# A two-layer graph network on one core: the last 32 chunks of layer 0 as two groups of 16, and a finished block's work inside its own group

## The chip, the cores and the metric

The kernel runs on 1 core of one Trainium2 chip. The metric is the device time of one execution in microseconds (us); the median of the runs is given. The core's engines are TensorE (PE; PEld is its weight load), VectorE (DVE), ScalarE (ACT), GpSimd (POOL) and SyncE (SP, here only DMA issues). Each runs its own instructions in order and waits on semaphores for the others.

## What is computed

There are 3750 nodes with 256 features and 120,000 edges in order of their target `dst`, which is uneven (3750 u^2). Two layers follow each other; in between only the residual `x` is kept.

```python
def _L0_gnn_ref(inputs, conv_weights, attn_l, attn_r, h_bias, edge_src, edge_dst, edge_type):
    feat_all = jnp.einsum('ni,rhid->rnhd', inputs, conv_weights)      # 8 relations, 4 heads of 64
    feat_src_e = feat_all[edge_type, edge_src]
    feat_dst_e = feat_all[edge_type, edge_dst]
    el = jnp.sum(feat_src_e * attn_l[edge_type], axis=-1)
    er = jnp.sum(feat_dst_e * attn_r[edge_type], axis=-1)
    e = jax.nn.leaky_relu(el + er, negative_slope=LEAKY_SLOPE)
    m = jax.ops.segment_max(e, edge_dst, num_segments=N_NODES)
    ex = jnp.exp(e - m[edge_dst])
    denom = jax.ops.segment_sum(ex, edge_dst, num_segments=N_NODES)
    alpha = ex / denom[edge_dst]
    h = jax.ops.segment_sum(alpha[..., None] * feat_src_e, edge_dst, num_segments=N_NODES)
    return h.reshape(N_NODES, OUT_FEAT) + h_bias
...
h = jnp.maximum(_layernorm(x, axis=-1), 0.0)
x = x + _L0_gnn_ref(h, L0_gnn_conv_weights, ..., src, dst, edge_type_8)
h = jnp.maximum(_layernorm(x, axis=-1), 0.0)
x = x + _L1_gnn_ref(h, src, dst, edge_type_8, ...)   # messages h @ W[type] summed by target, h @ loop_w, gelu, layernorm
```

## The kernel before

**Stages.** (1) The first norm, the features of every node for the 8 relations, stored as rows of `tab0`, and the tables of edges, sorted into chunks. (2) Layer 0 over the edges. (3) Layer 1 over the edges, from `tab1`. POOL's indirect DMAs (L843) fetch the rows of one chunk of 128 edges each.

**Layer 0.** The 30 blocks of 128 target nodes (`NB`) are in order of their number of edges, smallest first, and lie side by side in `ACC`. Their 996 chunks are taken in 32 groups (`GROUPS`): one of 4 chunks, 31 of `G` = 32. Two groups' rows fit into `Z` (`FE`), so POOL fetches one group while the engines work on the one before. `fetch` waits at chunks 0, 8, 16 and 24 of a group for semaphores of PE: select done (`s_es`), pairs done (`s_pair`), scores done (`s_sc`).

In one turn of the group loop, for group g:
- DVE, `attend(g)`: adds the two halves of the scores (`EV`, L1397), which needs the group's rows and select(g); PE transposes them (L2037); DVE scans for the maxima along the edges (L1410, L1412), PE transposes the two results (L2040), DVE scans over the chunks (RV, L1419, to L1448), PE spreads the result (L2044), DVE scans again, ACT takes Exp (EX, L1792), PE transposes it (L2048). With these weights `scale_rows` (L1383, 8 chunks at a time) multiplies the fetched rows.
- PE, `late`/`weigh` (L1889): one product with a one-hot matrix for each pair of chunks, into a ring of four PSUM banks (0, 1, 6, 7); a pair waits until DVE has added (`add`, L1355) the pair four before it into `ACC`. Pairs 0 to 3 of a group run in its own turn, 4 to 15 in the next turn, in the gaps of `attend`; `cuts(g)` says how DVE's adds are spread over them. `rescale` corrects the running sums of the block.
- For group g + 1: ACT turns the loaded targets into a one-hot (`turned`, two long activations) and copies the `er` rows (`stage`), PE makes `scores`, DVE picks the types (`types`, ERM, L1364), PE sums them (`select`, L1970), DVE makes one-hots (`onehot0`, L1373).
- Block r = g - 4 is finished (`finished_in`): DVE divides by the sums, adds bias and `x`, and norms it (`finish`, L1488 to L897, with the square root of ACT in between, L1631), ACT takes the Relu (`normed`, L1754). In the same turn PE flips it (`flip_block`, L1991, bank 3) and ACT moves it to `HT` (L1759). Its products with layer 1's weights (`block_products`: four quarters of 512 columns, L2006, in banks 2 and 3, then the own product L2009 to L2013) run a turn later, behind select; ACT moves each quarter to `ST1` (L1741) and the own product to `ACC` (L1746), SP stores the quarters into `tab1` (`store_table`).

PE's order at the end of a turn is: scores, pairs 0 to 3, select(g + 1), products of block r - 1, flip of block r. Behind the last group come block 26's leftovers, the turning back of layer 1's places (`TD`, `ERM`, fetched by 16 gathers of POOL, L858 and L859, once the last select is over), and blocks 27, 28 and 29, one behind the other. Layer 1's first gather waits for all stores into `tab1` and for `KI`.

## Time and profile before

| | us |
|---|---|
| runs (3): lowest, median, highest | 2775.06, 2777.38, 2780.21 |
| profiled execution, its own time | 2783.18 |
| its span, first to last instruction | 2781.4 |
| busy in the span: PE, DVE, ACT, POOL | 1935.2, 1523.3, 675.1, 2025.8 |
| mean granted TensorE clock | 0.809 of 2.4 GHz |

Shares and groups are of that one execution. In the rows below the first number is the start in us from the span's start, the second the time of the row in us; "xN" is the number of instructions merged in the row; the bracket at the end is the engine's idle time before it and what ended it. `Z` holds the gathered rows, `PB` is PSUM.

### The profile page before, as it was taken

Reading aid. Unit: us, or ns where it says so; the run is one execution under the profiler, and the core shown is the slowest. Engines: PE = TensorE matmul, PEld = TensorE weight load, DVE = VectorE, ACT = ScalarE, POOL = GpSimd, SP = SyncE. Lnnn points to the kernel's source line nnn. Section 1 sums busy time; section 2 is a strip of 40 time slices with the busy share of each in tenths; the row PEclk is TensorE's granted clock in tenths of the full one; section 3 lists DMA queues with packets and bytes.
Section 4 is the critical chain, followed back from the end, with each engine's and each line's share of the span. In section 5 each row is a group of like instructions: output and inputs, shape, how many; then the busy total and the mean of one; then the engine's idle time right before and its main releaser. Section 6 shows DMA issues by size and latency. Waiting matters only on the chain.

```text
span 2781.4 us, 26396 instructions
## 1 busy us (share of the span) xinstructions
PE 1935.2 (70%) x8092; PEld 1435.2 (52%) x8092; DVE 1523.3 (55%) x3170; ACT 675.1 (24%) x1248; POOL 2025.8 (73%) x2138
## 2 busy tenths in 40 slices
PE   7993567887878888798878556565555656556564
PEld 6982355555655555565555344444444444444443
DVE  7754677777778777777776333323332332333233
ACT  4653333444344434434432100000000000000001
POOL 5956777777777777777774577777777777777775
PEclk9995678889888988888899877768677676777767
DMA  8557455566665656565652533333333333333333
GB/s 244 206 192 223 145 146 166 168 171 178 179 169 166 185 166 176 170 181 168 170 162 86 163 105 105 105 110 106 110 105 110 111 105 110 106 110 109 107 112 93
DMA packets 168504, 403.11 MB, mean 145 GB/s; under 512 B 49741, under 2 KB 75820, under 8 KB 160682
## 3 DMA queue, kind: packets, MB, share of 16 engines
q0 software_dynamic: 95312, 261.58, 35.0%
q1 hardware_dynamic: 73050, 139.85, 14.5%
q8 instruction: 64, 1.05, 0.2%
q14 instruction: 78, 0.64, 0.1%
HBM read 325.41 MB, written 75.86 MB: 144 GB/s over the span
## 4 chain that ended last, share of the span: by engine, by line
POOL 58%; issue 19%; PE 11%; DVE 7%; DMA 2%; ACT 1%; DVEq 0%; POOLq 0%; SPq 0%; ACTq 0%
POOL Z L843 54%; PE PB L1889 4%; PE PB L2006 3%; DVE Z L1383 2%; DVE ACC L1355 2%; POOL ACC L804 2%; DMA Z<-tab,KI 1%; PE PB L1841 1%; POOL Z L807 1%; PE PB L1970 1%; POOL Z L801 0%; PE PB L2011 0%; DVE ERM L1364 0%; ACT L1631 0%; DMA Z<-in_L_gnn_basis 0%
## 5 line engine op out<-in xcount | busy, mean ns | idle before, releaser
L843 POOL DMA_INDIRECT Z<-tab,KI x1963 | 1866.6, 951 | 654.0 <-issue 591.6
L1889 PE MATMUL PB<-Z,OHZ 128*128 128x260 f32 (+1 forms) x3926 | 1199.2, 469 | 521.5 <-DMA Z<-tab,KI 392.2
L1889 PEld LDWEIGHTS PB<-Z,OHZ 128*128 128x128 f32 x3926 | 910.2, 239 | 756.4 <-DMA Z<-tab,KI 413.8
L1355 DVE TENSOR_TENSOR ACC<-ACC,PB 128x260 f32 (+1 forms) x997 | 421.7, 423 | 849.9 <-PE PB L1889 826.1
L1383 DVE TENSOR_TENSOR Z<-Z,PB 128x2048 f32<-128x2048 f32 (+1 forms) x125 | 284.1, 2273 | 0.0
L2006 PE MATMUL PB<-w,ht 128*128 128x512 f32 x480 | 267.6, 721 | 1.8 <-ACT ht L1759 1.8
L1970 PE MATMUL PB<-pick,ERM 128*128 128x16 f32 (+1 forms) x504 | 111.7, 371 | 171.0 <-DVE ERM L1364 171.0
L1970 PEld LDWEIGHTS PB<-pick,ERM 128*128 128x128 f32 (+1 forms) x504 | 108.3, 326 | 184.1 <-DVE ERM L1364 184.1
L1821 ACT ACTIVATE ACC<-ACC 128x256 f32<-128x256 f32 x30 | 10.4, 406 | 778.5 <-DVE ACC L1355 778.5
L2006 PEld LDWEIGHTS PB<-w,ht 128*128 128x128 f32 x480 | 111.1, 238 | 136.2 <-issue 133.6
L1719 ACT ACTIVATE OHZ<-OHZ,kid 128x4096 bf16<-128x4096 bf16 (+1 forms) x32 | 115.7, 3616 | 214.3 <-DMA OHZ<-dlt 214.3
L1841 PE MATMUL PB<-wh,hx 128*128 128x424 f32 (+1 forms) x500 | 146.4, 364 | 3.4 <-ACT hx L1645 3.4
L1373 DVE TENSOR_TENSOR OHZ<-DL,PB 128x1024 f32<-128x1024 bf16 (+1 forms) x122 | 140.1, 1210 | 0.1
L1565 DVE TENSOR_TENSOR OHZ<-DL,PB 128x4096 f32<-128x4096 bf16 (+1 forms) x31 | 133.6, 4311 | 0.0
L1741 ACT ACTIVATE st<-PB 128x512 f32<-128x512 f32 x120 | 68.3, 590 | 268.4 <-PE PB L2006 268.4
L1721 ACT ACTIVATE OHZ<-OHZ,ones 128x4096 bf16<-128x4096 bf16 (+1 forms) x32 | 115.7, 3615 | 1.0
L1631 ACT ACTIVATE sd<-ve 128x1 f32<-128x1 f32 (+2 forms) x52 | 10.6, 204 | 428.0 <-DVE ve L1588 403.1
L1841 PEld LDWEIGHTS PB<-wh,hx 128*128 128x128 f32 x500 | 95.8, 192 | 7.3 <-ACT hx L1645 4.9
L1841 PE MATMUL PB<-wx,hx 128*128 128x424 f32 (+1 forms) x250 | 90.2, 361 | 0.0
L1733 ACT ACTIVATE ERG<-ER 128x96 bf16 x498 | 88.8, 266 | 0.1
L1397 DVE TENSOR_TENSOR EV<-Z,PB 128x128 f32<-128x128 f32 (+1 forms) x32 | 11.8, 369 | 134.4 <-DMA Z<-tab,KI 133.1
L895 DVE RECIPROCAL rs<-sd 128x1 f32<-128x1 f32 (+2 forms) x41 | 6.8, 167 | 131.5 <-ACT sd L1631 131.5
(336 smaller groups left out, 1566.9 us busy)
## 6 DMA issues: line engine op xcount, KB each, us to landing
OHZ<-dlt SPq DMA_DIRECT2D x31, 1024.0 KB
Z<-tab,KI POOLq DMA_INDIRECT x1963, 2.8
tab<-st SPq DMA_DIRECT2D x120, 256.0 KB, 2.9
tab<-Z SPq DMA_DIRECT2D x24, 1040.0 KB, 4.0
TD<-typ SPq DMA_DIRECT2D x31, 256.0 KB
tab<-Z SPq DMA_DIRECT2D x5, 1024.0 KB, 7.4
xn<-xb SPq DMA_DIRECT2D x30, 128.0 KB, 2.3
X<-xn SPq DMA_DIRECT2D x6, 640.0 KB, 9.4
```

The source lines that it names most:

```text
L843: pool.indirect_dma_start(to, None, tab, at).then_inc(d_fe[g % 2][part(g, k) * layer], 16)
L1355: dv.tensor_tensor(a, a, bank(done + i)[:, 0:width], ALU.add).wait_op(*previous, "sem-ge").then_inc(*o.of(s_add))
L1373: dv.tensor_tensor(OH[:, 0, c:c + w, :], DL[:, k0 + c:k0 + c + w].unsqueeze(2).to_broadcast([128, w, 128]), (iob[:, :] if c and g == NG - ...
L1383: dv.tensor_tensor(f, f, weights.unsqueeze(3).to_broadcast([128, w, 4, HD]), ALU.mult).then_inc(*o.of(s_sr))
L1565: dv.tensor_tensor(OH[:, g % 2, 0:n, :], DL[:, k0:k0 + n].unsqueeze(2).to_broadcast([128, n, 128]), lanes.unsqueeze(1).to_broadcast([128, ...
L1719: ac.activation(d, d, ACT.Abs, bias=kid[:, 0:1], scale=-1.0).then_inc(*o.of())
L1721: ac.activation(d, d, ACT.Relu, bias=ones[:, 0:1], scale=-1.0).then_inc(*o.of())
L1733: ac.activation(ERG[:, q, :].rearrange("p (i r) -> p i r", i=3), ER3[:, :, bass.ds(at[q], 32)], ACT.Copy).then_inc(*o.of(s_eg if q == n // ...
L1841: last = pe.matmul(to, hx[:, 128 * c:128 * c + 128], parts[u](c), start=(i == 0 and c == 0 and u == 0), stop=(i == 1 and c == 1))
L1889: last = pe.matmul(p, OH[:, slot, k + i, :], rows_, start=(i == 0), stop=(i == n - 1))
L1970: last = pe.matmul(to, ERM[0:32 * parts, 128 * j:128 * j + 128], pick[0:32 * parts, 0:4 * parts].rearrange("p (a h) -> p a h", h=4), start ...
L2006: last = pe.matmul(quarter_bank(j)[:, :], HT[:, c, :], W1[:, c, 512 * j:512 * j + 512], start=(c == 0), stop=(c == 1))
```

## The change

1. The last 32 chunks of layer 0 are two groups of 16 (33 groups in all); block 27 is finished in the first of them. Groups of 16 load their masks in four pieces.
2. A block finished in group g has all its work in turn g: DVE's `finish` is cut in two, the first half behind `rescale`, the second behind the second scale_rows and its three adds; PE runs flip and four products ahead of select(g + 1) and the own product behind it, then waits for its move. The quarters use the pairs' banks 0, 6, 7 and 1.
3. Pairs 4 and 5 run at the end of their own turn (`early`); the other pairs are spread anew (6 and 7, 8, 9 to 12, 13 to 15). DVE's adds keep their cuts. POOL's waits come at chunks 0, 4, 8, 16 and 24.
4. Behind the last group: blocks 28 and 29 only, their products back to back (`LATE` = 28, with `HTL`, three buffers for the flipped block, two of them over `FW`/`BW` and `MX`/`ZR`), then the turning back; DVE copies `KI` from PSUM (before: ACT to `TDF`, then POOL), and the own products come last.
5. Masks: two more operations for each of the two new borders, in the first stage.

```diff
+CUT0 = KT * 128 - G // 2
+GROUPS = [(PAD, G - PAD)] + [(k, G) for k in range(G, KT * 128 - G, G)] + [(CUT0 - G // 2, G // 2), (CUT0, G // 2)]
...
-            return 0 if GROUPS[g][1] <= 8 else 9 if g == NG - 1 else 4
+            return 0 if GROUPS[g][1] <= 8 else 3 if g == NG - 1 else 4
 
         def cuts(g):
 
-            return (6, 10, 14) if g == NG - 1 else (5, 8, 11)
+            return 5, 8, 11
+
+        def early(g):
+
+            return 6 if 0 < g < NG - 2 else 4
...
-            return g - 4
+            return g - 4 if g < LATE + 4 else -1
 
         def product_of(r, j):
 
-            return 5 * NB + 5 * r + j + 1
+            return 5 * NB + (5 * r if r < LATE else 4 * r + LATE) + j + 1
+
+        def own_product(r):
...
+        def flip_bank(r):
+
+            return PB[4 if r >= LATE else 1]
+
+        def quarter_bank(r, j):
+
+            return PB[2 + j % 2 if r >= LATE else (0, 6, 7, 1)[j]]
+
+        def own_bank(r):
+
+            return PB[2 + r - LATE if r >= LATE else 0]
+
+        def flipped(r):
+
+            return HTL[max(r - LATE, 0)]
...
-                if 0 <= r and g < NG - 1:
+                if 0 <= r < LATE:
                     store_block(r)
-                    if r:
-                        store_table(r - 1)
                     load_block(r + 2)
+                    store_table(r)
...
+                            pool.wait_ge(s_pair, min(pair_no(g - 2, 4), pair_no(g - 1, 0)))
+                        elif k == 4:
                             pool.wait_ge(s_es, g)
                         elif k == 8:
                             pool.wait_ge(s_pair, min(pair_no(g - 2, 8), pair_no(g - 1, 0)))
                         elif k == 16:
+                            pool.wait_ge(s_pair, min(pair_no(g - 2, 12), pair_no(g - 1, 0)))
+                        elif k == 24:
                             pool.wait_ge(s_pair, pair_no(g - 1, 0))
-                        elif k == 24:
                             pool.wait_ge(s_sc, scored(g, 0))
...
-            pool.wait_ge(s_kt, VISITS + 4)
-            pool.tensor_copy(KI[:, :], TDF).then_inc(*o.of(s_loc))
 
             for j in range(4):
                 pool.wait_ge(d_st[j], 16 * NB)
-            pool.wait_ge(s_loc, 5)
+            pool.wait_ge(s_ki, 2)
...
-                norm_scale(r, r + 1, FIN + r)
+                dv.wait_ge(*o.last())
+                dv.tensor_scalar(ve[:, r:r + 1], mv[:, r:r + 1, 1], 1e-5, None, ALU.add).then_inc(*o.of(s_ve))
+                yield
+                dv.wait_ge(s_sd, no)
+                dv.reciprocal(rs[:, r:r + 1], sd[:, r:r + 1]).then_inc(*o.of())
+                dv.wait_ge(*o.last())
+                dv.scalar_tensor_tensor(nmr[:, r:r + 1], mv[:, r:r + 1, 0], -1.0, rs[:, r:r + 1], ALU.mult,
+                                        ALU.mult).then_inc(*o.of(s_nm))
...
+                norm = finish(finished_in(g)) if finished_in(g) >= 0 else iter(())
+                next(norm, None)
                 for c in range(8, n, 8):
+                    if g == NG - 1:
+                        onehot0(g, c)
                     scale_rows(g, c)
                     if c == 8 or g == NG - 1:
                         for q in range(3 * (c // 8 - 1), 3 * (c // 8)):
                             add(q0 + q, ROW0, 0)
                     elif c == 16:
                         add(q0 + 3, ROW0, 0)
+                    if c == 8:
+                        next(norm, None)
+                if n == G // 2 and g + 1 < NG:
+                    add(q0 + 3, ROW0, 0)
                 if g + 1 < NG:
                     types(g + 1)
-                for c in range(8 if g + 1 < NG else 24, n, 8):
-                    onehot0(g, c)
                 if g + 1 < NG:
+                    for c in range(8, n, 8):
+                        onehot0(g, c)
                     onehot0(g + 1, 0)
                     load_places(g + 1)
-                if finished_in(g) >= 0:
-                    finish(finished_in(g))
             for q in range(added_in_turn(NG - 1), GROUPS[NG - 1][1] // 2):
                 add(pair_no(NG - 1, q), ROW0, 0)
-            finish(NB - 2)
-            finish(NB - 1)
+            for r in range(LATE, NB):
+                for _ in finish(r):
+                    pass
+            for i in range(2):
+                dv.wait_ge(s_pt, VISITS + i + 1)
+                dv.tensor_copy(KI[:, 512 * i:512 * i + 512], PB[6 + i][:, :]).then_inc(*o.of(s_ki))
...
+                r = finished_in(g - 1)
+                if r >= 0:
+                    for j in range(4):
+                        move_quarter(r, j)
+                    move_own(r)
+                if g + 1 < NG:
                     stage(g + 1)
-                r = finished_in(g - 1)
-                if r > 0:
-                    move_quarter(r - 1, 0)
-                    move_quarter(r - 1, 1)
-                if r >= 0:
-                    normed(r)
-                if r > 0:
-                    move_quarter(r - 1, 2)
-                    move_quarter(r - 1, 3)
-                    move_own(r - 1)
-                if r >= 0:
-                    move_flipped(r)
                 ac.wait_ge(s_z, g + 1)
                 ac.activation(fe, fz, ACT.Exp).then_inc(*o.of(s_fx))
                 ac.wait_ge(s_zr, g + 1)
                 ac.activation(EX[0:R, :], ZR[0:R, :], ACT.Exp).then_inc(*o.of(s_xr))
-
-            last = finished_in(NG - 1)
-            for j in range(4):
-                move_quarter(last - 1, j)
-            move_own(last - 1)
-            normed(last)
-            ac.wait_ge(s_oh, batch_no(NG - 1, G))
-            for i in range(2):
-                ac.wait_ge(s_pt, VISITS + i + 1)
-                ac.activation(DL[:, 512 * i:512 * i + 512], PB[2 + i][:, :], ACT.Copy).then_inc(*o.of(s_kt))
+                r = finished_in(g)
+                if r >= 0:
+                    normed(r)
+                    move_flipped(r)
+
+            normed(LATE)
+            move_flipped(LATE)
+            for r in range(LATE, NB):
+                move_quarter(r, 0)
+                if r + 1 < NB:
+                    normed(r + 1)
+                move_quarter(r, 1)
+                move_quarter(r, 2)
+                if r + 1 < NB:
+                    move_flipped(r + 1)
+                move_quarter(r, 3)
...
-                if r == finished_in(NG - 1):
-                    pe.wait_ge(s_kt, VISITS + 2)
-                pe.transpose(PB[3][:, 0:128], H0[:, 1, 0:128], ident[:, :])
-                pe.transpose(PB[3][:, 128:256], H0[:, 1, 128:256], ident[:, :]).then_inc(s_tr, 1)
+                if r < LATE:
+                    pe.wait_ge(s_add, pair_no(r + 4, 1))
+                to = flip_bank(r)
...
+                    if r < LATE and j < 3:
+                        pe.wait_ge(s_add, pair_no(r + 4, j + 2))
+                    if r >= LATE and j > 1:
                         pe.wait_ge(s_ev, moved(r, j - 2))
+                    elif r > LATE:
+                        pe.wait_ge(s_ev, moved(r - 1, j + 2))
+                    if LATE <= r < NB - 1 and j == 3:
+                        flip_block(r + 1)
...
+            def own_product_of(r):
+
+                h, to = flipped(r), own_bank(r)
+                pe.wait_ge(s_ev, moved(r, 0) if r < LATE else moved(NB - 1, 3))
+                pe.matmul(to[:, 0:D], ones[0:1, :], HB1[:, :], start=True, stop=False)
                 for c in range(2):
-                    pe.matmul(PB[2][:, 0:D], HT[:, c, :], LWS[:, c, :], start=False, stop=False)
+                    pe.matmul(to[:, 0:D], h[:, c, :], LWS[:, c, :], start=False, stop=False)
                 for c in range(2):
-                    last = pe.matmul(PB[2][:, 128 * c:128 * c + 128], HT[:, c, :], ident[:, :], start=False, stop=(c == 1))
+                    last = pe.matmul(to[:, 128 * c:128 * c + 128], h[:, c, :], ident[:, :], start=False, stop=(c == 1))
                 last.then_inc(s_mm, 1)
+
+            def turn_back(tile, banks):
+
+                for i in range(2):
+                    for t in range(4):
+                        last = pe.transpose(banks[i][:, 128 * t:128 * t + 128], tile(4 * i + t), ident[:, :])
+                    last.then_inc(s_pt, 1)
...
+                late(g - 1, early(g - 1), 8)
                 pe.wait_ge(s_pk, g + 1)
                 pe.transpose(PB[5][0:1, 0:R], PK[0:R, 0:1], ident[0:R, 0:R])
                 pe.transpose(PB[5][0:1, 128:128 + R], PK[0:R, 1:2], ident[0:R, 0:R]).then_inc(s_row, 1)
-                late(g - 1, *cuts(g)[0:2])
+                late(g - 1, 8, 9)
                 pe.wait_ge(s_cf, g + 1)
                 pe.matmul(PB[4][0:R, 256:257], CF[:, 0, 0:R], ones[0:1, 0:1], start=True, stop=True)
                 pe.matmul(PB[4][0:R, 257:258], CF[:, 1, 0:R], ones[0:1, 0:1], start=True, stop=True).then_inc(s_cc, 1)
-                late(g - 1, *cuts(g)[1:3])
+                late(g - 1, 9, 13)
                 pe.wait_ge(s_xr, g + 1)
                 pe.transpose(PB[5][:, 256:256 + R], EX[0:R, :], ident[0:R, 0:R]).then_inc(s_wt, 1)
                 if g:
                     pe.wait_ge(s_fm1, g)
                     pe.matmul(PB[4][:, 400:404], OH[0:1, 0, 0, :], fm, start=True, stop=True).then_inc(s_ff, 1)
-                late(g - 1, cuts(g)[2], 16)
+                late(g - 1, 13, 16)
                 if g + 1 < NG:
                     scores(g + 1, 0)
                 late(g, 0, 3)
                 if g + 1 < NG and halves(g + 1) > 1:
                     scores(g + 1, 1)
                 late(g, 3, 4)
+                r = finished_in(g)
+                if 0 <= r < LATE:
+                    flip_block(r)
+                    block_products(r)
                 if g + 1 < NG:
                     select(g + 1)
-                r = finished_in(g)
-                if r > 0:
-                    block_products(r - 1)
-                if r >= 0 and g + 1 < NG:
-                    flip_block(r)
+                if 0 <= r < LATE:
+                    own_product_of(r)
+                    pe.wait_ge(s_own, r + 1)
+                if g + 1 < NG:
+                    late(g, 4, early(g))
             late(NG - 1, 4, 16)
-
-            last = finished_in(NG - 1)
+            flip_block(LATE)
+            block_products(LATE)
+            block_products(LATE + 1)
             pe.wait_ge(s_loc, 4)
-            pe.wait_ge(s_own, last)
-            pe.wait_ge(s_ev, moved(last - 1, 3))
-            for i in range(4):
-                for t in range(4):
-                    tile = TD[:, 4 * i + t, :] if i < 2 else ERM[:, 512 * (i - 2) + 128 * t:512 * (i - 2) + 128 * t + 128]
-                    last = pe.transpose(PB[2 + i][:, 128 * t:128 * t + 128], tile, ident[:, :])
-                last.then_inc(s_pt, 1)
-
-            for r in range(finished_in(NG - 1), NB):
-                flip_block(r)
-                block_products(r)
-
             pe.wait_ge(s_add, NPAIR)
+            turn_back(lambda t: ERM[:, 128 * t:128 * t + 128], (PB[6], PB[7]))
+            turn_back(lambda t: TD[:, t, :], (PB[0], PB[1]))
+            for r in range(LATE, NB):
+                own_product_of(r)
```

## Rows read from the trace of the kernel before

**Rows 1.** Head of the page, and engines' shares of the chain that ended last
```profile
span 2781.4 us, 26396 instructions
...
POOL 58%; issue 19%; PE 11%; DVE 7%; DMA 2%; ACT 1%; DVEq 0%; POOLq 0%; SPq 0%; ACTq 0%
```

**Rows 2.** Waits: who waited for whom, us in total, times, longest
```profile
POOL Z L843 <- issue: 591.6, 1940, 0.3
```

**Rows 3.** Timeline of POOL: layer 0's first gather, the index gathers, layer 1's first
```profile
219.44 1.03 POOL L843 DMA_INDIRECT Z<-tab,KI  x1 [25.19 <-DMA tab<-Z]
...
1473.08 0.95 POOL L858 DMA_INDIRECT TD<-sdst,offi  x1 [0.31 <-issue]
...
1553.51 0.98 POOL L843 DMA_INDIRECT Z<-tab,KI  x1 [29.95 <-DMA tab<-st]
```

**Rows 4.** Timeline of a group in the body, first part, DVE and PE
```profile
1195.31 0.38 DVE L1397 TENSOR_TENSOR EV<-Z,PB 128x128 f32<-128x128 f32 x1 [2.79 <-DMA Z<-tab,KI]
...
1196.07 0.33 PE L2037 MATMUL PB<-IDX,E 128*128 128x128 f32 x1
...
1204.48 4.65 PE L1889 MATMUL PB<-Z,OHZ 128*128 128x260 f32 x20
...
1205.17 2.28 DVE L1383 TENSOR_TENSOR Z<-Z,PB 128x2048 f32<-128x2048 f32 x1
...
1210.34 2.29 DVE L1383 TENSOR_TENSOR Z<-Z,PB 128x2048 f32<-128x2048 f32 x1
...
1212.66 1.34 DVE L1355 TENSOR_TENSOR ACC<-ACC,PB 128x260 f32 x3
...
1213.46 1.14 PE L1889 MATMUL PB<-Z,OHZ 128*128 128x260 f32 x4
```

**Rows 5.** Timeline of the same group, second part
```profile
1220.23 3.59 PE L1970 MATMUL PB<-pick,ERM 128*128 128x16 f32 x16 [5.62 <-DVE ERM L1364]
...
1223.66 9.77 PE L2006 MATMUL PB<-w,ht 128*128 128x512 f32 x16
...
1224.73 0.18 DVE L1488 TENSOR_SCALAR dn<-ACC 128x4 f32<-128x4 f32 x1
...
1227.29 0.15 DVE L893 TENSOR_SCALAR ve<-mv 128x1 f32<-128x1 f32 x1
...
1232.18 0.16 DVE L895 RECIPROCAL rs<-sd 128x1 f32<-128x1 f32 x1 [4.74 <-ACT sd L1631]
...
1232.57 0.60 ACT L1754 ACTIVATE H<-xb,nmr,rs 128x256 f32<-128x256 f32 x1 [0.42 <-DVE nmr L897]
...
1233.71 0.69 PE L2009 MATMUL PB<-hb1s,ones 1*128 1x256 f32 x2 [0.28 <-ACT st L1741]
...
1235.94 0.39 ACT L1746 ACTIVATE ACC<-PB 128x256 f32<-128x256 f32 x1 [1.80 <-PE PB L2013]
```

**Rows 6.** Windows: length, busy of PE, PEld, DVE, ACT, POOL, then PEclk, DMA, GB/s
```profile
1218.00:1220.00 2.00, 0.00 (x0) 0.00 (x0) 2.00 (x3) 2.00 (x13) 1.39 (x3) 0.70 0.30 92
1220.00:1222.00 2.00, 1.77 (x9) 1.77 (x9) 2.00 (x3) 0.62 (x4) 1.60 (x2) 0.50 0.51 133
...
1229.00:1230.00 1.00, 1.00 (x4) 0.52 (x3) 0.00 (x0) 0.00 (x0) 0.69 (x2) 0.99 0.73 172
```

**Rows 7.** Timeline from the last group to the last product, DVE, PE and ACT
```profile
1475.73 0.37 DVE L1397 TENSOR_TENSOR EV<-Z,PB 128x128 f32<-128x128 f32 x1 [3.27 <-DMA Z<-tab,KI]
...
1519.99 0.43 DVE L1355 TENSOR_TENSOR ACC<-ACC,PB 128x260 f32 x1 [0.45 <-PE PB L1889]
...
1532.80 7.13 PE L2006 MATMUL PB<-w,ht 128*128 128x512 f32 x16 [0.53 <-ACT ht L1759]
...
1541.79 0.14 PEld L1991 LDWEIGHTS PB<-IDX,H 128*128 128x128 f32 x1
...
1542.81 7.13 PE L2006 MATMUL PB<-w,ht 128*128 128x512 f32 x16 [0.53 <-ACT ht L1759]
...
1549.98 0.60 ACT L1741 ACTIVATE st<-PB 128x512 f32<-128x512 f32 x1 [1.12 <-PE PB L2006]
```

81 lines of the change are left out of this document (30 added, 51 removed).

## The prediction

> **What bounds the kernel now.** I read the page's head and chain first [rows 1]: GpSimd (POOL) alone is 58% of the chain that ended last, and "issue" 19%. The waits put a name to that 19%: before 1940 of the 1963 gathers POOL waited for nothing but its own issue, 591.6 us, 0.305 each [rows 2]. POOL's timeline then cuts the run into three parts behind the first stage [rows 3]: layer 0's 996 gathers from 219.44 to 1473.1 us, 1.26 us each; a hole to 1553.51 us, in which POOL does 16 short gathers of indices and at last waits 29.95 us for a store of `tab`; then layer 1, gathers again. A group of 32 chunks takes POOL about 40.1 us, and DVE still has to wait 2.79 us for its last gathered row when it begins one [rows 4]. So the body of layer 0 goes at POOL's pace. A changed kernel can gain only in the hole of 80.4 us. It can lose there, and in the body if another engine comes to need more than 40.1 us for a group.
>
> **The body: a block's work inside its own group.** I cost it along one path. Let PE's transposes of the scores (L2037, 1196.07) be 0.
> (a) To the first scale_rows: 1205.17 - 1196.07 = 9.1 us now [rows 4]. In the new order two pairs of 0.93 us stand ahead of the row transposes instead of one (20 matmuls are 5 pairs in 4.65 us), and pair 12, now ahead of the transposes of EX, has to wait until DVE has added pair 8. I take 1.2 us for both: 10.3.
> (b) scale_rows, five adds, rescale (1205.17 to 1210.34) [rows 4]: 15.5.
> (c) The first half of finish comes here: 1224.73 to 1227.44, 2.7 us [rows 5]: 18.2.
> (d) scale_rows 2.3, three adds 1.35 [rows 4]: 21.9. The square root falls under it.
> (e) Reciprocal to the end of the Relu, 1232.18 to 1233.17, 1.0 us [rows 5]: 22.9.
> (f) Turning the block and moving it out, 1541.79 to 1542.81, and a semaphore, 1.1 us [rows 7]: 24.0.
> (g) Four products: 7.0 us at 2.4 GHz (7.13 in the row) [rows 7]. At 1.2 GHz each matmul takes twice as long, so every us spent at that clock adds half a us.
> (h) select, now behind them: 3.4 us between its start and the products', at a granted clock of 0.50 [rows 5, 6]. No row has it at the full clock; it can't be under half, 1.7, nor over 3.4. I take 2.1, nearer to half, because the products' matmuls do halve.
> (i) Own product and its move: 1233.71 to 1236.33, 2.6, with a semaphore 2.7 [rows 5]. PE now waits for this move; queued behind the wait are pairs 4 and 5 and the next group's transposes.
> (j) Pairs 4 and 5: 1.9 us.
> Sum: 24.0 + 7.0 + 2.1 + 2.7 + 1.9 = 37.7 us, plus half of the time at the low clock. Now PE stands still from 1214.6 to 1220.23, 5.62 us; the clock falls within 1218 to 1220, and is back at 1229.0, 5.3 us into the products [rows 4 to 6]. In the new order PE stands still for about 3.4 us, so the clock may fall or not: 0 to 5.3 us cold give 37.7 to 40.4, the middle 39.3. POOL's 40.1 still ends last, by 0.8 us. The path of the present order, worked out the same way (select at 24.1, products, own product, flips), needs 40.0, so the new one is no longer.
> What hides the rest: the quarters' moves on ACT wait behind the two long activations of turned() and end under select, since each quarter has a bank of its own. SP issues the table's stores in the same turn, behind the loads of masks, steps and targets and not in front of them, and the next masks are asked for only after the next transposes. POOL's waits come at chunks 0, 4, 8, 16 and 24; the tightest is select's, some 5 us ahead of its gather. Should the cover of 0.8 us go, its price is the excess times 27 groups. Body: 0; ends -2 (POOL's few short waits gone) and, with select at 3.4 us and the clock always low, 27 x 1.6 = +43 us.
>
> The clock is the doubtful term: the 3.4 us of select left it at 0.50, and it rose under the products [rows 5, 6]. The Trainium skill, "TensorE: Matmul & The Clock Gate", section "HAM oscillation — how this bites in real kernels", says that a loop in which the array waits in each turn restarts throttled in each turn. By that rule the products start cold in every group, which is the 40.4 of the sum and 0.3 us over POOL's pace; by the bare sum it is 37.7. The rule speaks against this change, which puts a wait for DVE and ACT right ahead of the dearest matmuls.
>
> **The hole: two groups of 16.** The last group of before starts at 1475.73 [rows 7]; the first of the two gets PE at about 1475.9.
> First group of 16: block 27 is finished in it, so its path is (a) to (i) again, 37.7 - 1.9, less 0.6 for vectors of half the width in (a) (an estimate: five or six short operations, 0.1 each), plus 1.6 for the clock: **36.8 us**. Half the chunks save gathers, half of the scale_rows, and pairs 4 and 5. DVE could go on near 28 us, but the next group's select stands behind block 27's products.
> Second group of 16: transposes to scale_rows 9.1 + 2.4 (four pairs ahead of the row transposes) - 0.9 = 10.6; scale_rows 2.3, rescale 0.6, a one-hot 1.2, scale_rows 2.3, three adds 1.35; pairs 4 to 7 at 0.9 each end 3.5 later: 21.8. PE idles for most of the first 13 us, so 1.0 for a low clock: **22.8 us**.
> From the last add to block 28's products: 2.7 of (c), 0.3 for the square root (an estimate, as long as a semaphore and a small operation of the rows), (e) and (f): 5.1. Products of 28 and 29 to the start of the last move: 7.35 (with the flip of 29 inside) + 7.17 (1542.81 to 1549.98) [rows 7] = 14.5. PE has stood still for 5 us before them: 4.4 us cold, 2.2. The move 0.6; from its end, 1550.58, to POOL's gather at 1553.51, 2.9 [rows 3, 7].
> Sum: 1475.9 + 36.8 + 22.8 + 5.1 + 14.5 + 2.2 + 0.6 + 2.9 = 1560.8 against 1553.5: **+7.3 us**. In words: now the last add starts at 1519.99 and three blocks of 10.0 us follow (1532.80 to 1542.81) [rows 7]. One block of the three goes, and 3.0 us between the others, but the last add comes 15 us later.
> Other queues: POOL's 16 index gathers wait for the last select, so they start near 1510 instead of at 1473.08 and are issued by 1530, 20 us early. DVE's two copies of the indices stand behind block 29's products; at 0.6 us each (the nearest row, a move of 512 columns) they end 1.3 us before the last store lands, and would be the bound at 1.3 us each. The masks' four new operations lie in the first stage. Ends of the hole: no cold clock at all, 4.8 less, +2.5; select at 3.4 us and up to twice the cold time, +12.
>
> **The time.** The profiled run took 2783.18 us, its span 2781.4 [rows 1]; the median of the runs shown is 2777.38, 5.8 less. With body 0 and hole +7.3 the profiled execution would take 2790.5 and the median is **2784.7**.
>
> **Rivals.**
> A, the body is lost to PE: select at 3.4 us, or the low clock coming back over pairs 4 to 7 after select, lifts a group over 40.1. It decides from 2.4 us beyond 37.7. At 0.5 to 1.5 us in 27 groups it gives +14 to +40 and, with the hole, 2798 to 2825. For it: the small slack. Against it: the present order has none by the same sum and holds POOL's pace.
> B, **faster**: the first group of 16 is not serial. If it takes under 24 us instead of 36.8, the hole shrinks by over 5.5 us: 2767 to 2772; break-even is 29.5. For it: the rows have landed long before, DVE could go on at 28 us, and 10.0 us of block 27 are really gone. Against it: PE's order is fixed, products, select, own product, and block 27's Relu would have to come 9 us earlier than in (e).
> C, within 0.2%: the clock stays high over the short waits, and the hole grows by 2.5 to 5 us: 2780 to 2782.5.
>
> **How the numbers follow.** About 0.2% (5.5 us) is what a measurement of this kernel can tell from no change. Forecast, +5.5 to +12: 0.40. C, with the small sums around it: 0.26. A: 0.20. B: 0.14. Hence faster 0.14, same 0.26, slower 0.60. The likeliest case alone reaches from 2783 to 2790. The range takes in much of A and B: 2772 to 2806.
>
> **What would show it.** Right, if: the gathers of layer 0 still follow each other at 1.25 us and end near 1473; L1397 is still released by gathered rows and not by select (else A); the products start about 24 us after the transposes; the last two groups' transposes are 37 us apart (B: 24); the last add is near 1535; two blocks follow instead of three; layer 1's first gather is near 1561 and released by a table store. Wrong, if the 37 us are not there, or if layer 1 waits for the indices.

## The result, and the profile after

The kernel before takes 2778.80 us beside it (4 runs, 2775.06 to 2783.59), the changed one 2807.76 us (4 runs, 2804.65 to 2810.87): ratio 1.010, 95% interval 1.0086 to 1.0114. The change costs 29 us, four times the forecast of 7.3, and lies just outside the range (2806). A second measurement gave the same ratio (g1_change, below). Rival A has come about in its size and its mark, on top of the hole that was forecast.

The profiled execution took 2805.64 us, its span is 2803.9. First the shares of the chain that ended last, of after; they answer to [rows 1]:

```profile
span 2803.9 us, 26507 instructions
...
POOL 37%; PE 30%; DVE 16%; issue 14%; ACT 2%; DMA 1%; DVEq 0%; POOLq 0%; SPq 0%; ACTq 0%
POOL Z L864 37%; PE PB L2033 10%; PE PB L1918 10%; PE PB L1870 5%; DVE Z L1405 5%; DVE ACC L1377 4%; PE PB L1994 2%; PE PB L2043 1%; PE PB L2041 1%; ACT H L1789 1%; PE PB L2045 0%; PE PB L2014 0%; DVE xb L1523 0%; DVE st L1525 0%; DVE H L1515 0%
```

POOL fell from 58% to 37% of the chain, PE rose from 11% to 30%; the products (L2033) and the pairs (L1918) are 10% each. The waits of after (who waited for whom, us in total, times, longest) say at which place; they answer to [rows 2] and to the wait in the first of [rows 4]:

```profile
DVE EV L1419 <- DMA Z<-tab,KI: 66.5, 10, 12.3
DVE EV L1419 <- PE PB L1994: 62.7, 23, 9.4
POOL Z L864 <- PE PB L1918: 34.4, 40, 9.1
POOL Z L864 <- issue: 585.4, 1919, 0.6
```

EV is DVE's first operation of a group. Before, the group's last gathered row released it [rows 4]; now in 23 groups it is select (L1994), which stands behind the finished block's products. The prediction named this very line as the mark of rival A.

A turn of after, PE's timeline (start us, us, engine, line, operation, out<-in, count, and what ended the idle time before). It answers to [rows 4, 5]:

```profile
1162.54 0.27 PE L2076 MATMUL PB<-IDX,E 128*128 128x128 f32 x1
...
1166.77 0.38 PE L2083 MATMUL PB<-ones,CF 1*128 1x1 f32 x2 [1.02 <-DVE CF L1459]
...
1167.91 5.46 PE L1918 MATMUL PB<-Z,OHZ 128*128 128x260 f32 x16 [0.54 <-DVE ACC L1377]
1173.21 0.27 PE L2087 MATMUL PB<-IDX,EX 128*128 128x128 f32 x1
...
1186.70 0.47 PE L2014 MATMUL PB<-IDX,H 128*128 128x128 f32 x1 [3.18 <-ACT H L1789]
1186.97 0.42 PE L2015 MATMUL PB<-IDX,H 128*128 128x128 f32 x1
1187.86 9.49 PE L2033 MATMUL PB<-w,ht 128*128 128x512 f32 x16 [0.47 <-ACT ht L1794]
1197.19 1.85 PE L1994 MATMUL PB<-pick,ERM 128*128 128x16 f32 x16
1198.97 0.69 PE L2041 MATMUL PB<-hb1s,ones 1*128 1x256 f32 x2
...
1201.64 2.02 PE L1918 MATMUL PB<-Z,OHZ 128*128 128x260 f32 x8 [0.47 <-ACT ACC L1781]
1203.50 0.27 PE L2076 MATMUL PB<-IDX,E 128*128 128x128 f32 x1
```

From transposes to transposes 40.96 us: 25.3 to the products, 9.3 to select, 1.8, 2.7 to pairs 4 and 5, 1.9. From group 13 on, seventeen turns in a row have 41.0 us each, to 0.1; before, the turns of the 30 full groups have 40.3 us in the mean and vary from 39.4 to 41.8. The windows of this turn (columns as in [rows 6]) show the clock:

```profile
1162.54:1185.90 23.36, 18.26 (x115) 13.49 (x113) 19.30 (x52) 5.01 (x16) 17.29 (x19) 0.93 0.57 168
1185.90:1192.60 6.70, 5.43 (x8) 2.45 (x9) 6.67 (x7) 5.74 (x4) 4.99 (x6) 0.50 0.49 133
1192.60:1203.50 10.90, 10.43 (x45) 6.83 (x45) 4.97 (x9) 6.13 (x13) 8.35 (x9) 1.00 0.67 200
```

TensorE stood still for 3.18 us ahead of the flip; the granted clock is 0.50 (1.2 GHz) from 1185.9 to 1192.6 and 1.00 (2.4 GHz) from there on, so 4.7 of the products' 9.3 us are at the lower level. DVE's timeline in the next turn gives step (a):

```profile
1214.79 0.16 DVE L1488 TENSOR_SCALAR F<-PB 128x4 f32<-128x4 f32 x1 [2.00 <-PE PB L2090]
...
1215.07 2.28 DVE L1405 TENSOR_TENSOR Z<-Z,PB 128x2048 f32<-128x2048 f32 x1
```

1215.07 - 1203.50 = 11.6 us from the transposes to the first scale_rows; 9.1 before [rows 4].

The clock is low a second time in the turn, and that time lies inside (a). Here is the stretch that holds most of pairs 9 to 12, first in the turn shown and then in a turn that begins at 713.20, in which the clock stayed high (columns as in [rows 6]); below them PE's rows for the same four pairs in that second turn, and DVE's first scale_rows:

```profile
1168.74:1172.16 3.42, 3.42 (x10) 2.65 (x9) 2.88 (x10) 1.59 (x2) 2.79 (x3) 0.50 0.48 104
718.60:722.60 4.00, 3.76 (x16) 2.99 (x17) 3.65 (x11) 1.50 (x2) 3.09 (x4) 1.00 0.48 103
```

```profile
718.57 2.90 PE L1918 MATMUL PB<-Z,OHZ 128*128 128x260 f32 x12 [0.54 <-DVE ACC L1377]
721.71 1.12 PE L1918 MATMUL PB<-Z,OHZ 128*128 128x260 f32 x4 [0.24 <-DVE ACC L1377]
...
723.56 2.28 DVE L1405 TENSOR_TENSOR Z<-Z,PB 128x2048 f32<-128x2048 f32 x1
```

At 2.4 GHz the 16 matmuls take 4.3 us (718.57 to 722.83), with a wait of 0.24 inside; in the turn above, at 0.50 for 3.4 us, they take 5.46. And 723.56 - 713.20 = 10.4 us is (a) at the full clock. That turn has 39.7 us in all, though its products are as slow (9.51).

The hole of after, all engines; it answers to [rows 3, 7]:

```profile
1524.80 1.95 PE L1994 MATMUL PB<-pick,ERM 64*128 64x8 f32 x16
...
1527.02 0.95 POOL L879 DMA_INDIRECT TD<-sdst,offi  x1 [23.10 <-PE PB L1994]
...
1530.82 0.30 PE L2076 MATMUL PB<-IDX,E 128*64 128x128 f32 x1 [0.47 <-ACT ACC L1781]
...
1553.13 0.42 DVE L1377 TENSOR_TENSOR ACC<-ACC,PB 128x260 f32 x1 [0.45 <-PE PB L1918]
...
1558.57 6.75 PE L2033 MATMUL PB<-w,ht 128*128 128x512 f32 x12 [0.47 <-ACT ht L1794]
...
1574.15 0.60 ACT L1776 ACTIVATE st<-PB 128x512 f32<-128x512 f32 x1 [1.12 <-PE PB L2033]
...
1577.68 0.97 POOL L864 DMA_INDIRECT Z<-tab,KI  x1 [26.18 <-DMA tab<-st]
```

The transposes of the first group of 16 are at 1491.9. From there to layer 1's first gather it takes 85.8 us, where before takes 77.0 from the last group's transposes (1476.5): the hole lost 8.8 us. Between the two spans (2781.4 and 2803.9, 22.5 apart) the books are: body of layer 0 +21.0, hole +8.8, the stage ahead of layer 0 -5.6 (its first gather is at 213.85 instead of 219.44, which nothing in the change explains), layer 1 -1.7. The medians are 29 apart, since that first stage varies: in g1_change, the same kernel, layer 0's first gather is at 218.6.

### The profile page after: what moved, and what is told of

It is laid out like the page before. It is cut to its first block, busy times and chain, and to the rows that moved or that the text cites. A ratio compares the mean times of both kernels' runs of the same rounds, so it can differ in the third digit from the quotient of the medians.

```text
span 2803.9 us, 26507 instructions
## 1 busy us (share of the span) xinstructions
PE 1982.6 (71%) x8118; PEld 1444.1 (52%) x8118; DVE 1535.0 (55%) x3206; ACT 678.3 (24%) x1252; POOL 2029.7 (72%) x2137
## 4 chain that ended last, share of the span: by engine, by line
POOL 37%; PE 30%; DVE 16%; issue 14%; ACT 2%; DMA 1%; DVEq 0%; POOLq 0%; SPq 0%; ACTq 0%
POOL Z L864 37%; PE PB L2033 10%; PE PB L1918 10%; PE PB L1870 5%; DVE Z L1405 5%; DVE ACC L1377 4%; PE PB L1994 2%; PE PB L2043 1%; PE PB L2041 1%; ACT H L1789 1%; PE PB L2045 0%; PE PB L2014 0%; DVE xb L1523 0%; DVE st L1525 0%; DVE H L1515 0%
## 5 line engine op out<-in xcount | busy, mean ns | idle before, releaser
L1918 PE MATMUL PB<-Z,OHZ 128*128 128x260 f32 (+1 forms) x3926 | 1268.1, 487 | 570.0 <-DMA Z<-tab,KI 378.5
L1918 PEld LDWEIGHTS PB<-Z,OHZ 128*128 128x128 f32 x3926 | 941.6, 248 | 840.9 <-DMA Z<-tab,KI 403.6
L2033 PE MATMUL PB<-w,ht 128*128 128x512 f32 x464 | 273.1, 754 | 13.7 <-ACT ht L1794 13.7
L1850 ACT ACTIVATE ACC<-ACC 128x256 f32<-128x256 f32 x30 | 10.4, 406 | 773.5 <-DVE ACC L1377 773.5
L2033 PEld LDWEIGHTS PB<-w,ht 128*128 128x128 f32 x464 | 111.4, 247 | 161.8 <-issue 137.0
L1666 ACT ACTIVATE sd<-ve 128x1 f32<-128x1 f32 (+2 forms) x52 | 10.6, 203 | 709.4 <-DVE ve L1623 402.7
L1754 ACT ACTIVATE OHZ<-OHZ,kid 128x4096 bf16<-128x4096 bf16 (+2 forms) x33 | 115.7, 3507 | 49.6 <-DMA OHZ<-dlt 49.6
L1756 ACT ACTIVATE OHZ<-OHZ,ones 128x4096 bf16<-128x4096 bf16 (+2 forms) x33 | 116.0, 3514 | 1.1
L1994 PEld LDWEIGHTS PB<-pick,ERM 128*128 128x128 f32 (+2 forms) x520 | 68.4, 206 | 35.5 <-DVE ERM L1386 21.6
L1419 DVE TENSOR_TENSOR EV<-Z,PB 128x128 f32<-128x128 f32 (+2 forms) x33 | 11.9, 360 | 129.1 <-DMA Z<-tab,KI 66.5
L1994 PE MATMUL PB<-pick,ERM 128*128 128x16 f32 (+2 forms) x520 | 66.7, 270 | 19.6 <-DVE ERM L1386 19.6
L2014 PE MATMUL PB<-IDX,H 128*128 128x128 f32 x30 | 13.5, 449 | 93.3 <-ACT H L1789 93.3
L1776 ACT ACTIVATE st<-PB 128x512 f32<-128x512 f32 x120 | 65.7, 591 | 44.1 <-PE PB L2033 43.7
## 6 DMA issues: line engine op xcount, KB each, us to landing
X<-xn SPq DMA_DIRECT2D x6, 640.0 KB, 10.3
```

The lines of the kernel that those rows point to most:

```text
L1754: ac.activation(d, d, ACT.Abs, bias=kid[:, 0:1], scale=-1.0).then_inc(*o.of())
L1756: ac.activation(d, d, ACT.Relu, bias=ones[:, 0:1], scale=-1.0).then_inc(*o.of())
L1918: last = pe.matmul(p, OH[:, slot, k + i, :], rows_, start=(i == 0), stop=(i == n - 1))
L1994: last = pe.matmul(to, ERM[0:32 * parts, 128 * j:128 * j + 128], pick[0:32 * parts, 0:4 * parts].rearrange("p (a h) -> p a h", h=4), start ...
L2033: last = pe.matmul(quarter_bank(r, j)[:, :], flipped(r)[:, c, :], W1[:, c, 512 * j:512 * j + 512], start=(c == 0), stop=(c == 1))
```

## Experiments

The theory after the first look, which knew nothing of the second low stretch: the order inside a group makes a path on PE and DVE of 41.0 us, 0.9 over the 40.1 us that the prediction gives POOL; two terms are to blame, (a) and the clock under the products, and either one's removal brings POOL's pace back. The rival: something else about the new order costs (a loaded engine, an awkward release of Z), or the halves slow the body down too.

**e1_spread**: the changed kernel with pair 12 put back behind the transposes of EX. In later expectations this is called the earlier finish, or slots 9 and 12.

```diff
-                late(g - 1, 9, 13)
+                late(g - 1, 9, 12)
...
-                late(g - 1, 13, 16)
+                late(g - 1, 12, 16)
```

> One edit to the changed kernel: pair 12 goes back behind the transposes of EX (pairs 9 to 11 before them, 12 to 15 behind). Path theory: a turn of the engines takes 41.0 us in the changed kernel, POOL's gathers 40.1; pair 12 has to wait for DVE's add of pair 8 and holds up the first scale_rows, which comes 11.6 us after the score transposes instead of 9.1. Then the scale_rows come at about 10.3, the turn needs 39.7, POOL's pace bounds the body again, and some 0.9 us x 27 turns = 18 to 24 us go: 2784 to 2790 against 2807.8. Clock theory: the turn is 41.0 because of the 4.8 us at the low clock in the products; the wait saved is lost again to a longer low clock, the turn stays within 0.3 us of 41.0, and the time within 5 us of 2807.8. Hole theory (the 29 us are lost in the two groups of 16): no change either, with turns of 41.0.

Measured: 2786.2 us beside 2776.8 (9 runs), ratio 1.0032 (1.0022 to 1.0043). PE's timeline in a turn that begins at 1155.84:

```profile
1161.13 4.54 PE L1918 MATMUL PB<-Z,OHZ 128*128 128x260 f32 x12 [0.49 <-DVE ACC L1377]
1165.51 0.27 PE L2087 MATMUL PB<-IDX,EX 128*128 128x128 f32 x1
...
1180.03 9.57 PE L2033 MATMUL PB<-w,ht 128*128 128x512 f32 x16 [0.47 <-ACT ht L1794]
1189.44 1.85 PE L1994 MATMUL PB<-pick,ERM 128*128 128x16 f32 x16
```

Products start 24.2 us after the transposes and are still slow, 9.4 us to select; this turn has 39.9 us, and the full turns have 40.3 us in the mean, as before. DVE's EV is released by gathered rows in 30 groups. Step (a) is 10.2 us in the mean, and of two kinds: 10.6 where the clock was low in it, 9.4 where not. So one pair ahead of EX's transposes is worth 1.0 us a turn, with the low clock left in place. Of what is left over before, 9.4 us, the hole has 5.2: 82.2 us.

**e2_warm**: the changed kernel with ten matmuls, whose result is not used, ahead of the flip, to fill TensorE's wait. The rest of the computation is unchanged.

```diff
+                    for _ in range(10):
+                        pe.matmul(PB[4][:, 260:388], ident[:, :], W1[:, 0, 0:128], start=True, stop=True)
                     flip_block(r)
```

> One edit to the changed kernel: ten matmuls of 128 columns whose result nobody reads are put in front of the flip of blocks 0 to 27, where PE stands still for 3.2 us. Clock theory: the clock no longer falls there, the products take 7.0 instead of 9.3 us, the turn needs 38.7 us and falls to POOL's 40.1: 2784 to 2790 against 2807.8, mean granted clock in the body near 1.0 instead of 0.87. Path theory without the clock: the filler costs nothing and gives nothing, 2807 to 2809. If the filler ends after the Relu it delays the flip by up to 1 us a turn: 2810 to 2835.

Measured: 2780.74 us (10 runs), ratio 1.0018 (1.0007 to 1.003), 27 us under the changed kernel. PE's timeline in a turn that begins at 1151.43:

```profile
1172.11 2.39 PE L2101 MATMUL PB<-w,IDX 128*128 128x128 f32 x20
1175.31 0.33 PE L2014 MATMUL PB<-IDX,H 128*128 128x128 f32 x1 [0.81 <-ACT H L1789]
...
1176.22 7.13 PE L2033 MATMUL PB<-w,ht 128*128 128x512 f32 x16 [0.47 <-ACT ht L1794]
...
1191.80 0.33 PE L2076 MATMUL PB<-IDX,E 128*128 128x128 f32 x1 [2.12 <-DVE E L1422]
```

The filler (the trace counts each matmul twice) is 2.39 us of work in a wait of over 3; the products take 7.13 us in every turn of the body. The turn is 40.4 us and ends with 2.1 us of waiting for DVE: the path is 38.2, half a us beside the 37.7 of the prediction's bare sum. Step (a) is still 11.6 in most turns, and the low stretch in it is still there: the granted clock is 0.68 over pairs 9 to 12 (1156.7 to 1162.0). The mean granted clock from 400 to 1400 us is 0.97, against 0.88. So the clock under the products, too, is enough by itself.

**e3_one32**: the new order inside a group, but one last group of 32, as before.

```diff
-GROUPS = [(PAD, G - PAD)] + [(k, G) for k in range(G, KT * 128 - G, G)] + [(CUT0 - G // 2, G // 2), (CUT0, G // 2)]
+GROUPS = [(PAD, G - PAD)] + [(k, G) for k in range(G, KT * 128, G)]
```

> The changed kernel with one last group of 32 chunks, as before, instead of two of 16; block 27 is still finished in it, all else of the change stays. Hole theory as I costed it: the two groups of 16 take 38.9 + 22.7 us from transposes to last add; one group of 32 takes about 37.4 (block 27 inside) and then pairs 4 to 15, 12 x 0.9, so 50: about 11 us less, 2795 to 2799 against 2807.8, with the body's turns still 41.0. If most of the 29 us came from the two groups of 16: 2780 to 2787. If the half groups are free: 2806 to 2809.

Measured: 2796.58 us (4 runs), ratio 1.0076 (1.006 to 1.0093). Its turns settle at 41.0 us as well (21 in a row), EV is released by select in 24 groups, and the hole is 77.2 us against the 77.0 of before: finishing block 27 inside a last group of 32 gains nothing, since the last add comes 52.6 us after the transposes (43.5 before). The order inside a group is the part that costs 20 us, and the halves the 9 of the hole.

**e4_ownfirst**: the changed kernel with the own product ahead of select, so that its move runs under select.

```diff
                     block_products(r)
+                    own_product_of(r)
                 if g + 1 < NG:
                     select(g + 1)
                 if 0 <= r < LATE:
-                    own_product_of(r)
                     pe.wait_ge(s_own, r + 1)
```

> One edit to the changed kernel: in a turn the own product runs ahead of select, so that its move by ACT (0.38 us and two semaphores, 0.75 us in all) lies under select and PE no longer stands still for it. Path theory: the turn gets 0.75 us shorter, 40.2 to 40.3, so 0.7 x 27 = about 19 us go: 2787 to 2792. Clock theory: the turn keeps near 41.0 and the time is within 5 us of 2807.8. It costs something if select, now 2.6 us later, becomes what POOL or the next attention waits for: 2808 to 2815.

Measured: 2787.91 us (4 runs), ratio 1.0046 (1.0029 to 1.0063), full turns of 40.3 us in the mean, hole 84.8. A third way to take a us off the path, with the same effect.

**The same ideas where everything is slower.** In the next two batches the kernel before takes 3469 and 3473 us. Whether that belongs to a chip isn't known: the first of them ran on chip 9 and the second on chip 8, but e1 to e4 are down as chip 8 as well, and there the kernel before took 2777. e5_one32_short and f5_one32_short are the same kernel (e3 with the edits of e1 and e4); e6_three_late and f6_three_late leave block 27 to the end as well; e7_three_late_warm is three late blocks with the filler of e2 in place of the edits of e1 and e4; e8_halves_three_late and f8_halves are e6 with halves.

```diff
-        LATE = NB - 2
+        LATE = NB - 3
```

> The changed kernel with three edits together: one last group of 32 (as e3), pair 12 behind the transposes of EX (as e1), own product ahead of select (as e4). It asks what the own-group order is worth once the body is held at POOL's pace. Path theory: turns of 40.1 (path 39.0), hole as in e3, 77 us from the last score transposes to layer 1's first gather, as in the kernel before: 2773 to 2780, the same as the kernel before within 0.2%. If the gains of e1 and e4 don't go with e3's group: above 2785.

> e5 with block 27 left out of the last group: blocks 27, 28 and 29 follow the last add, their products back to back. Nothing but pairs is then left for PE in the last group. Path theory: the last add comes about 34 to 37 us after the last score transposes (43.5 in the kernel before, 52.6 in e3), then 5.0 to the first products, 22.8 for three blocks, 0.6 and 2.9: 65 to 69 us instead of 77, so 8 to 12 us under the kernel before: 2765 to 2770. If POOL's 16 index gathers, their turning back or the copies of the indices are the bound instead: 2771 to 2776.

> e6's tail with e2's means for the body: the ten unused matmuls ahead of the flip instead of the two shorter waits (pair 12 and the own product stay as in the changed kernel). Clock theory: the body holds POOL's pace as in e2, mean granted clock 0.97, and the time is that of e6 within 5 us, 2765 to 2772. If the filler's 3.0 us get in front of a flip: 5 to 15 us above e6.

> The changed kernel with e1's and e4's edits and block 27 taken out of the first group of 16 (three blocks behind the last add, as in e6), the two groups of 16 kept. It prices the halves by themselves. Path theory: the first half's select follows the types, so the second half's score transposes come 26 to 28 us after the first's instead of 38.9; then 22.7 to the last add, 5.0, 22.8, 3.5: 80 to 83 us from the transposes of the first half to layer 1's first gather, 12 to 15 us above e6: 2779 to 2784. Rival B of the prediction (halves overlap and win): at or below e6.

> One last group of 32; inside the group the finish of the block starts earlier (slots 9 and 12) and the own product stands before the select, so that the path has some 2 us less than in the kernel after and the turn is POOL's again (39.9 to 40.1 us). The blocks 27, 28 and 29 are all left to the end: the last group carries no products, no select and no own move, and three blocks of products run at the end instead of two. Path theory: last transposes to the last add 52.6 us less the work of a block that has left PE (some 12 us), of which POOL's 32 gathers of 1.25 us leave at least 40.1: hole from the transposes of the second to last group to the gather of layer 1 of 69 to 73 us against 77; body as before. Sum 2765 to 2772 us, ratio 0.996 to 0.998. Rival, the third block's products and moves (16 matmuls, 4.7 to 9.5 us by the clock) stand on the path to the first gather of layer 1: 2775 to 2781 us.

> The same, but block 27 is finished in the last group, as in the one with one last group of 32, and two blocks are left to the end: nothing but the order inside a group is changed against the kernel before. Path theory: the turn is POOL's, 39.9 to 40.1 us, since the path (41.0 us when the products run at the low clock) has lost 1.9 us by the earlier finish and the own product before the select; hole 77 us as before: 2775 to 2781 us, ratio 0.999 to 1.001. Rival, the work inside a group costs more than its path (DVE or PE more loaded, each group's last pairs later): turns of 40.5 us and more, 2790 to 2797 us.

> The short order inside a group and the three blocks left to the end, with the last 32 chunks as two groups of 16: it differs from the one with three late blocks by the halves alone. Path theory: the second group of 16 can't start its gathers' adds before the first is done, and its own first part (transposes to first scaling, some 11 us, and the first additions behind it) is paid a second time: 6 to 10 us more than with one last group of 32: 2773 to 2781 us. Rival, the halves cost nothing by themselves once no block is finished in the first of them: within 2 us of the one with three late blocks.

Measured: e5 3296.85 (ratio 0.9493, 0.9462 to 0.9523), e6 3295.07 (0.9481, 0.9454 to 0.9508), e7 3448.71 (0.995, 0.9919 to 0.9981), e8 3301.25 (0.9517, 0.948 to 0.955); f6 3300.92 (0.9497), f5 3295.90 (0.9509), f8 3297.09 (0.9505), their intervals 0.9461 to 0.9553 together. None of these expectations could be met there, for they are sums over POOL's pace, and there POOL has no share of the chain that ended last (0% in e6, 61% in g2). Waits of e6 (columns as above), and then 1000 us of layer 1 in e6 and in g2, which is e6 at the ordinary speed (columns as in [rows 6]):

```profile
POOL Z L866 <- issue: 555.8, 1820, 1.1
POOL Z L866 <- remote: 257.5, 73, 6.3
```

```profile
1950.00:2950.00 1000.00, 458.33 (x1364) 327.31 (x1364) 271.89 (x467) 22.80 (x36) 665.24 (x704) 0.65 0.33 94
```

```profile
1700.00:2700.00 1000.00, 585.69 (x1601) 447.52 (x1601) 326.57 (x562) 32.40 (x51) 756.49 (x800) 0.74 0.37 108
```

A gather keeps POOL busy for 0.95 us in both, but POOL issues 704 of them in 1000 us of layer 1 instead of 800, and over the whole execution it waits 257.5 us for something that the profile can only call remote. The packets of the gathers' queue are not slower: they take 29.0% of 3302.3 us in e6 and 34.7% of 2758.1 us in g2, 958 and 957 us. What the traces do show is that other engines go on late after TensorE. ACT's move of the flipped block waits for nothing but the flip; the waits for it in e7 and in g2:

```profile
ACT ht L1793 <- remote: 168.5, 27, 9.4
```

```profile
ACT ht L1793 <- PE PB L2014: 19.9, 28, 0.8
```

and one turn of e7, PE and ACT:

```profile
1499.67 0.27 PE L2014 MATMUL PB<-IDX,H 128*128 128x128 f32 x1
...
1508.77 0.38 ACT L1793 ACTIVATE ht<-PB 128x256 f32<-128x256 f32 x1 [9.32 <-remote]
1509.21 9.96 PE L2032 MATMUL PB<-w,ht 128*128 128x512 f32 x16 [9.27 <-ACT ht L1793]
```

The flip's last matmul ends at 1499.94 by the profile (the ends of matmuls are modelled), and ACT starts 8.8 us later; in the other direction PE follows ACT within 0.1 us. Whether the matmul really ended late or its signal came late, and why, isn't in the profile, and it stays open. So does what g1's expectation, below, supposes, that gathers land later there: these traces give no landing times for them.

The kernels of these batches can be compared with each other, but the path does not explain the differences. The full turns of e7 have 56.1 us in the mean, those of e6 51.0, and the two differ in the edits of e1 and e4 against a filler, 154 us in all. By the path of the ordinary speed they should be within a us of each other (38.2 with the filler, about 39 with the two edits). ACT's waits for the flip are 169 us in e7 in all and 50 in e6, which is most of the difference; why they are longer behind the filler isn't shown. Halves or not, two late blocks or three, can't be told apart there. Why the kernel before is 170 us slower than e6 there isn't shown either: no trace of it was taken there.

**The questions at the ordinary speed.** g1_change is the changed kernel, g2_three_late is e6, g3_short is e5.

> The change as it stands. If the kernel before takes 2777 us here, the same 2805 to 2809 us as first measured (turn locked at 41.0 us). If it takes about 3470 us here: gathers then land later, POOL waits for Z and is no longer the pace; path theory: what counts is how soon after a block's products the Z slots come free, and the own-group order alone gives most of what the short orders gave there (3296): 3300 to 3330 us. Rival: the gain there came from the short order (earlier finish, own product first), and the change alone gives nothing: 3450 to 3490 us.

> Three blocks left to the end, one last group of 32, short order inside a group. At 2777 us for the kernel before: 2765 to 2772 us, since the last group of 32 loses the work of a block and is held by POOL's 32 gathers (at least 40.1 us) instead of 52.6 us, while a third block of products runs behind it; rival, the third block's 5 to 9 us stand on the path and nothing is gained: 2775 to 2781 us. At 3470 us for the kernel before: 3300 us, as measured.

> The kernel before with the order inside a group alone, in its short form. At 2777 us for the kernel before: path theory 2775 to 2781 us (turn 39.9 to 40.1 us, last groups as before); rival, the order costs more than its path: 2790 to 2797 us. At 3470 us for the kernel before: 3296 us, as measured.

Measured beside 2773.91 us for the kernel before: g1_change 2802.32 (4 runs, 1.010, 1.0079 to 1.0121), g2_three_late 2767.75 (10 runs, 0.9975, 0.9964 to 0.9986), g3_short 2770.19 (10 runs, 0.999, 0.9979 to 1.0001).

g1_change locks at 41.0 us again, twenty turns in a row from group 10 on. g3_short has the new order inside a group, shortened by 2 us, and one last group of 32; what the change does behind the last group (point 4) is still in it, though its expectation speaks of nothing but the order. Its full turns have 40.2 us, no loss: the order itself costs nothing beyond its path; that was open until here. The kernel before was 3 us faster in this batch than the 2777 of the expectation; by its ratio, 0.999, g3 lies at the lower end of the path theory's 0.999 to 1.001. Its hole is 74.2 us, 2.8 less than before and 3.0 less than in e3, which lacks the edits of e1 and e4.

g2_three_late beats the kernel before by 0.25% (0.14% to 0.36%). Its last group, and what follows, PE, DVE and POOL:

```profile
1467.05 0.94 POOL L881 DMA_INDIRECT TD<-sdst,offi  x1 [0.60 <-PE PB L1993]
...
1469.40 0.33 PE L2075 MATMUL PB<-IDX,E 128*128 128x128 f32 x1 [0.78 <-DVE E L1421]
...
1503.11 0.43 DVE L1376 TENSOR_TENSOR ACC<-ACC,PB 128x260 f32 x1 [0.45 <-PE PB L1917]
...
1508.74 6.96 PE L2032 MATMUL PB<-w,ht 128*128 128x512 f32 x12 [0.47 <-ACT ht L1793]
...
1535.14 0.97 POOL L866 DMA_INDIRECT Z<-tab,KI  x1 [43.37 <-DMA tab<-st]
```

The last add starts 33.7 us after the transposes, where e3, which finishes a block in that group, takes 52.6; three blocks of products follow, and the hole is 65.7 us, under my expected 69 to 73. I had bounded the last group by POOL's 40.1 us, wrongly: the index gathers start at 1467.05, so all its rows were issued before its transposes. The hole is 8.5 us shorter than g3's, but the medians of the two are only 2.4 us apart and their runs overlap (2759.7 to 2770.3 and 2767.8 to 2778.1). The profiled execution is g2's fastest one; where the rest goes in its other runs wasn't seen and stays open.

## Why the prediction was wrong

The steps of the body, by the turn shown above:

- (a), 10.3 us, was too short by 1.3: 11.6. This is the first step that failed, and what it lacked is a term for the clock. The sum has the clock in (g) alone; in (a) it stands at nothing, without a reason. The order itself was priced well: at the full clock (a) is 10.4 us (the turn at 713.20). In 25 of the 26 turns from group 5 on the granted clock is 0.50 for 3.4 us inside (a), while pairs 9 to 12 run, and (a) has 11.6 us in the mean. TensorE had stood still twice just before the clock fell, for 1.02 and 0.54 us; it did so in the turn at 713.20 too, where the clock stayed high, and what tells the two apart isn't shown. DVE's pace costs little there: PE waits 0.24 us for a bank within the four pairs. e1 and e2 show the same two kinds of turn, 1.2 us apart: 10.6 and 9.4 with one pair less, 11.6 and 10.4 with the filler.
- (b) to (f) carry that 1.3 us along and add none: products 25.3 us after the transposes where 24.0 was said.
- (g), 7.0 us at the full clock and half of the cold time on top, is right as a rule: 9.3 = 7.0 + 4.7 / 2, and e2 has 7.13. What failed is the value taken for the cold time. The sum took 1.6 us for it, as if the clock fell or not from turn to turn. It called that the middle of 0 to 5.3 us cold, which is 1.3, so that the 39.3 should have been 39.0. The cold time was 4.7 us, near the upper end, in nearly every turn: 2.4 us, 0.8 more than was taken. The prediction had the argument in hand: the Trainium skill, "TensorE: Matmul & The Clock Gate", section "HAM oscillation — how this bites in real kernels", says that a loop whose array waits in each turn starts cold in each turn. The trace agrees: 0.50 at the products' start in this turn, and products of 9.48 to 9.52 us in all locked turns of g1_change. I weighed the rule, and gave it too small a chance.
- (h), select, was bounded by 1.7 and 3.4 us and taken at 2.1: it is 1.8, since the clock is back by then. Gain 0.3. (i) 2.7 and (j) 1.9 were right.

Sum: 39.3 + 1.3 + 0.8 - 0.3 = 41.1, measured 41.0, over the 40.4 that the prediction gave for all of 5.3 us cold. POOL's pace was a little slower than said, too: 40.3 us for a full turn of before, short waits included, not 40.1. The products' clock alone would have left 39.8, under that pace; the turn at 713.20 is this case, with 39.7. (a) alone, with the value taken for the products, gives 40.3, at the pace. The two together are 0.7 us over it, and 30 full turns make the 21 us. Rival A had put its price at 0.5 to 1.5 us and its time at 2798 to 2825; measured 2808. Its number came true, not its mechanism: select took 1.8 us and not 3.4, and the clock was low over pairs 9 to 12 of the group before and over the products, not behind select. The chance of 0.20 was too small for a cover of 0.8 us under a sum of ten terms, one of which had a range of 2.7 us by itself.

The hole: +8.8 us against +7.3. First group of 16, 38.9 us for 36.8: here (a) was as priced, 9.7, but the products took 9.6 us to select for 8.6, and the own product and its move 4.1 for 2.7, at a granted clock of 0.57 (1527 to 1531). From its successor's transposes to the end of the last add 22.7 for 22.8, to block 28's products 5.0 for 5.1, to the start of the last move 15.6 for 16.7 (less of them cold), 0.6, and 2.9. The index gathers started at 1527.0, behind the last select as said, and their end came 28 us ahead of the first gather, which a table store released. Rival B would have needed 24 us for the first group; it took 38.9. Of the marks set in the prediction, those of the hole were met up to 2 us, counted from the first group's transposes. Those of the body were not: layer 0's gathers ended at 1503 and not near 1473, EV was released by select, and the products started 1.3 us late.

## What to carry to other kernels

When one engine is the pace of a loop and the other engines' path is moved, sum that path to the end and ask not whether it is longer than the pace in the middle of the ranges, but what the cover is beside the terms' ranges: a cover of 0.8 us under a path with a term of 0 to 2.7 us is no cover. A wait put right ahead of the largest matmuls of each turn (3.2 us here) should be priced at the low clock in all turns, and the granted clock should be read over the whole turn: here it was low at a second place, where the sum had no term for it. A few unused matmuls in the wait, or a us taken off anywhere on the path, bought back 20 to 27 us here. And work left to the end of a stage can take less time than the same work in its last group, if the inputs of that group have long arrived: g2's hole is 8.5 us shorter than g3's in the profiled executions, though the medians differ by 2.4 only.

## What the runs showed of the hardware

The turn locks: in the changed kernel and in e3 each turn has the same length to 0.1 us, the granted clock falls and rises at the same two places in each (from 6.2 to 9.6 and from 23.3 to 30.1 us after the transposes in the turn shown), and the products take 9.5 us each time. In the kernels at POOL's pace (e1, g3) they vary from 8.4 to 10.0 us between turns, and gathered rows, not select, release EV in 30 and 31 groups. The time at the low clock is no more than before, 10.1 us a turn in both kernels; what changed is that in most turns of before it was one stretch, which began while TensorE stood still ahead of select, and afterwards there are two.

In two batches all these kernels took a fifth to a quarter longer, with the same time for each instruction but for TensorE's clock (a gather 0.95 us, an add 0.42 us), and other engines went on up to 9 us late behind TensorE. There the shortened orders are 5% faster than the kernel before instead of 0.1 to 0.3%. The path of the ordinary speed does not say why.
